# Fetching a unit of queries and keys in six transfers of 24 or 48 rows in place of twelve of 16

## The reference

```python
x = x + attn(layernorm(x))        # 16 heads, two softmaxes over 8-wide q, k; a1 @ v - lam * a2 @ v, rms norm, W_proj
x = x + xattn(layernorm(x), ctx)  # one head of 256, gelu, residual
x = x + ffn(layernorm(x))         # shared SwiGLU of 1024, and 2 of 16 routed experts of 256
```

## Time and profile before

| | |
|---|---|
| median of 3 runs | 569.85 us (569.31 to 571.27) |
| the profiled execution | 569.25 us, of which 568.0 us are the span |
| PE busy | 537.7 us (95%) |
| mean granted TensorE clock | 0.976 of 2.4 GHz |
| DVE, ACT, POOL busy | 311.8, 260.1, 228.0 us |
| queue of SP and ACT | 58,688 packets, 61.11 MB, 37.8% of 16 engines' span |

### The profile page before, as it was taken

The page is one execution under the profiler, slowest core; times in us unless marked ns, Lnnn a source line. Parts: engine busy times, 40 slices in busy tenths (PEclk is TensorE's granted clock), DMA queues, the critical chain, the costliest instruction groups (busy, mean ns, idle before and its releaser), DMA issues.

```text
span 568.0 us, 10919 instructions
## 1 busy us (share of the span) xinstructions
PE 537.7 (95%) x3792; PEld 374.1 (66%) x3792; DVE 311.8 (55%) x685; ACT 260.1 (46%) x420; POOL 228.0 (40%) x473
## 2 busy tenths in 40 slices
PE   8989878988999997799999999999999999999998
PEld 7544434645547564665585466467999999999547
DVE  5868875898898975885242762112222222222284
ACT  7335654654574664526512200102666666666110
POOL 2444766576645444523010024563244444444200
PEclk9989978999998999799999999999999999999999
DMA  7873483346431319920039806122233333332372
GB/s 238 245 177 122 116 249 92 112 124 182 135 114 43 103 55 147 310 58 0 0 112 349 281 28 211 69 90 88 75 94 95 92 90 92 95 94 83 129 280 75
DMA packets 62725, 72.99 MB, mean 129 GB/s; under 512 B 14832, under 2 KB 55792, under 8 KB 61136
## 3 DMA queue, kind: packets, MB, share of 16 engines
q1 hardware_dynamic: 58688, 61.11, 37.8%
q0 software_dynamic: 3792, 10.39, 5.2%
q10 hardware_dynamic: 192, 0.79, 0.6%
HBM read 45.84 MB, written 26.03 MB: 127 GB/s over the span
## 4 chain that ended last, share of the span: by engine, by line
PE 80%; DVE 6%; SPq 5%; ACT 3%; issue 3%; DMA 2%; POOL 1%; ACTq 0%; DVEq 0%; POOLq 0%
PE ps L671 18%; PE ps L739 15%; PE ps L682 10%; PE ps L750 7%; PE ps L399 5%; PE ps L467 3%; PE ps L595 3%; PE ps L416 2%; PE ps L455 2%; PE ps L572 2%; PE ps L548 2%; SPq L1885 2%; DVE nmax L949 2%; PE ps L695 2%; PE ps L728 2%
## 5 line engine op out<-in xcount | busy, mean ns | idle before, releaser
L949 DVE TENSOR_REDUCE nmax<-ps 128x8 f32<-128x1024 f32 x64 | 77.6, 1217 | 26.1 <-PE ps L434 24.8
L739 PE MATMUL ps<-xt,Wn 128*128 128x128 f32 x752 | 91.8, 275 | 0.1
L739 PEld LDWEIGHTS ps<-xt,Wn 128*128 128x128 f32 x752 | 87.7, 192 | 0.4 <-ACT xt L1549 0.3
L1729 POOL DMA_INDIRECT y_rows<-yo,goes_to x47 | 45.8, 975 | 82.0 <-DVE yo L1218 81.7
L1445 ACT ACTIVATE prob<-ps 128x1024 f32<-128x1024 f32 x64 | 65.4, 1021 | 24.7 <-PE ps L455 24.6
L1210 DVE TENSOR_TENSOR ht<-sa,ps 128x256 f32<-128x256 f32 x47 | 19.8, 422 | 99.2 <-PE ps L750 95.2
L1542 ACT ACTIVATE sil<-ps 128x512 f32<-128x512 f32 x32 | 19.1, 597 | 115.2 <-PE ps L671 115.2
L671 PE MATMUL ps<-xT,W1s 128*128 128x512 f32 x128 | 60.6, 596 | 1.6 <-ACT sil L1542 0.9
L671 PE MATMUL ps<-xT,W2s 128*128 128x512 f32 x128 | 60.2, 592 | 0.0
L682 PE MATMUL ps<-W3s,hTs 128*128 128x256 f32 x256 | 56.1, 380 | 0.8 <-DVE hTs L1141 0.8
L1562 ACT ACTIVATE Wn<-W 128x1024 f32 x47 | 49.7, 1057 | 12.6 <-issue 12.6
(11 more groups left out here) (186 smaller groups left out, 830.2 us busy)
## 6 DMA issues: line engine op xcount, KB each, us to landing
W<-in_L_ffn_routed_w_dram SPq DMA_DIRECT2D x12, 1024.0 KB, 11.8
pack_q<-qk_parts SPq DMA_DIRECT2D x48, 128.0 KB, 3.1
xg<-x_slots SPq DMA_DIRECT2D x47, 129.0 KB, 2.1
x_slots<-zero SPq DMA_DIRECT2D x11, 512.0 KB, 10.6
qk_parts<-part SPq DMA_DIRECT2D x21, 256.0 KB, 3.1
pack_k<-qk_parts SPq DMA_DIRECT2D x42, 128.0 KB, 3.1
yg<-y_rows SPq DMA_DIRECT2D x4, 1024.0 KB, 8.6
Cx<-in_ctx_dram SPq DMA_DIRECT2D x5, 512.0 KB, 4.3
```

Of the source, the lines that this page charges most:

```text
L739: r = t.matmul(ps[:, 2 + p, h * P:(h + 1) * P], Wn[:, n % 3, k, h * P:(h + 1) * P], xt[:, p, k, :], start=(k == 0), stop=(k == KT - 1))
L949: v.tensor_reduce(nmax[:, s % 4, a, :, :], ps[:, b:b + 2, :].rearrange("p m (h t) -> p m h t", h=4), AX_X, ALU.max, negate=True).then_inc( ...
L1729: g.indirect_dma_start(out=y_rows, out_offset=bass.IndirectOffsetOnAxis(ap=goes_to[:, n:n + 1].bitcast(U32), axis=0), in_=yo[:, p, :], in_ ...
```

## The change

The slots are laid out anew. Queries are stored as first, first, second, third part, and keys mirrored as third, second, first, first, in the slots 0 to 3. Queries' rows then are slots 0, 1, 2 and slots 1, 2, 3; keys' rows are slots 1, 2, 3 and slots 0, 1, 2, and the six products come out as before. For a group, the queries are one transfer of 48 rows whose source is a hand-built access pattern of [2 x 24 x one row], with a step of one slot in the outer dimension, so that two slots are read twice; its destination is 48 partitions. The keys of a group are two transfers of 24 rows each. A unit is fetched by 2 + 4 = 6 transfers. The first part of the queries is now stored twice, so a chunk has eight stores. The fetch is cut in `fetch_queries` and `fetch_keys`: units 3 to 7 are fetched in two steps in place of three, queries (two transfers) in the first and keys (four) in the next; unit 2 whole in step 1; the queries of unit 0 are all issued behind the second parts of half 1, ahead of its third parts.

```diff
-PARTS_AT = (((0, 1), (2, 0), (2, 2)), ((0, 2), (2, 1)), ((0, 0), (2, 3)))
-Q_RUNS = [1, 1, 0]
-K_RUNS = [0, 1, 2]
+PARTS_AT = ((0, 1), (2,), (3,))
+SLOTS, RUNS = 4, 3
-PIECES = len(Q_RUNS) + len(K_RUNS)
-FETCHES = 2 * PIECES
-STORES = 7
+FETCHES = 6
+STORES = 8
...
+        def half_of_group(pack, m, i):
+            lo = MG * m + i * RUNS * HD
+            return pack[lo:lo + RUNS * HD, :, :].rearrange("p h t -> p (h t)")
+        def keys_places(c, half, m, i):
+            return qk_parts[c, 2 + half, 1 - i:1 - i + RUNS, :, m * HU:(m + 1) * HU, :].rearrange("q d h t -> (q d) (h t)")
+        def queries_places(c, half, m):
+            first = qk_parts[c, half, 0, 0, m * HU, :]
+            return bass.AP(first.tensor, first.offset, [[HD * MU * CT, 2], [MU * CT, RUNS * HD], [1, HU * CT]])
...
-                for f0, at_ in PARTS_AT[i]:
-                    q.dma_start(qk_parts[c, f0:f0 + 2, at_, :, :, :].rearrange("f d m t -> (d m) f t"),
-                                part[PART_OF[c]][:, i, f0:f0 + 2, :]).then_inc(parts_stored[c], 16)
+                for place in PARTS_AT[i]:
+                    for f0, at_ in ((0, place), (2, SLOTS - 1 - place)):
+                        q.dma_start(qk_parts[c, f0:f0 + 2, at_, :, :, :].rearrange("f d m t -> (d m) f t"),
+                                    part[PART_OF[c]][:, i, f0:f0 + 2, :]).then_inc(parts_stored[c], 16)
...
-                            q.dma_start(tile[MG * m + r0:MG * m + KQ:3, :, :].rearrange("p h t -> p (h t)"),
-                                        qk_parts[c, f, p0:p0 + 2, :, m * HU:(m + 1) * HU, :].rearrange(
-                                            "q d h t -> (q d) (h t)")).then_inc(packed[u], 16)
+            def fetch_queries(unit):
+                c, half, u = unit // 2, unit % 2, unit % UNITS
+                may_fetch(unit)
+                for m in range(2):
+                    q.dma_start(Qp[u][MG * m:MG * m + KQ, :, :].rearrange("p h t -> p (h t)"),
+                                queries_places(c, half, m)).then_inc(packed[u], 16)
+            def fetch_keys(unit):
+                c, half, u = unit // 2, unit % 2, unit % UNITS
+                may_fetch(unit)
+                for m in range(2):
+                    for i in range(2):
+                        q.dma_start(half_of_group(Kp[u], m, i), keys_places(c, half, m, i)).then_inc(packed[u], 16)
...
-            fetch(0, range(1))
+            fetch_queries(0)
             store_half(1, 2)
-            fetch(0, range(1, len(Q_RUNS)))
             store_part(1, 0)
-            fetch(1, range(3))
+            fetch_queries(1)
             put_max(0)
-            fetch(1, range(3, PIECES))
+            fetch_keys(1)
...
-                if s in (1, 2):
-                    fetch(2, range(3 * (s - 1), 3 * (s - 1) + 3))
-                if CB <= s and s // CB + UNITS - 1 < STEPS // CB and s % CB < 3:
-                    fetch(s // CB + UNITS - 1, range(2 * (s % CB), 2 * (s % CB) + 2))
+                if s == 1:
+                    fetch_queries(2)
+                    fetch_keys(2)
+                if CB <= s and s // CB + UNITS - 1 < STEPS // CB and s % CB < 2:
+                    (fetch_queries, fetch_keys)[s % CB](s // CB + UNITS - 1)
```

More of the change, by code:

```diff
@@ L1418, in fetch_keys @@
                 a.wait_ge(halves_stored[half], 16 * STORES)
[L1419 to L1423, removed]
+                for m in range(2):
+                    for i in range(2):
+                        a.dma_start(half_of_group(Kp[unit], m, i), keys_places(0, half, m, i)).then_inc(packed[unit], 16)
             def put_values(c, i):
@@ L1859, in store_part, with may_fetch @@
                 q.wait_ge((firsts, seconds, thirds)[i], 4 * (c + 1))
-                for f0, at_ in PARTS_AT[i]:
-                    q.dma_start(qk_parts[c, f0:f0 + 2, at_, :, :, :].rearrange("f d m t -> (d m) f t"),
-                                part[PART_OF[c]][:, i, f0:f0 + 2, :]).then_inc(parts_stored[c], 16)
+                for place in PARTS_AT[i]:
+                    for f0, at_ in ((0, place), (2, SLOTS - 1 - place)):
+                        q.dma_start(qk_parts[c, f0:f0 + 2, at_, :, :, :].rearrange("f d m t -> (d m) f t"),
+                                    part[PART_OF[c]][:, i, f0:f0 + 2, :]).then_inc(parts_stored[c], 16)
             def store_half(half, i):
-                for n, (f0, at_) in enumerate(PARTS_AT[i]):
-                    f = f0 + half
+                for f, mirrored in ((half, False), (half + 2, True)):
                     q.wait_ge((firsts, seconds, thirds)[i], ORDER.index(f) + 1)
[L1868 to L1872, removed]
+                    for place in PARTS_AT[i]:
+                        at_ = SLOTS - 1 - place if mirrored else place
+                        q.dma_start(qk_parts[0, f, at_, :, :, :].rearrange("d m t -> (d m) t"),
+                                    part[0][:, i, f, :]).then_inc(halves_stored[half], 16)
+            def may_fetch(unit):
+                c, half = unit // 2, unit % 2
                 if unit < UNITS:
```

## The result

The changed kernel takes 674.77 us (median of 4 runs, 673.2 to 675.44), against 569.58 us of the kernel before (median of 4, 566.8 to 571.27): a ratio of 1.185, 95% interval 1.180 to 1.190, or 105 us more. Forecast were 640 us, in a range of 585 to 677. The direction and the mechanism were right; the growth was forecast a third too small (70 us for 105). The forecast's own range, 615 to 670, is missed by 5 us: the time lies inside the wide one only because that reached to 677 for a rival that did not come true.

What follows compares the result with a forecast made beforehand. PE bounds the kernel, busy 537.7 of 568.0 us. Stalls of 46.7 + 12.4 + 15.8 = 74.9, less 8, plus 3 for the clock, on 569.25 give 639.2, rounded to 640 us; own range 615 to 670, overall 585 to 677.

Steps and rivals of the forecast that it cites:

- Few engines: Attention fetches: a queries' transfer, (48, 2), runs on 2 engines with 24 rows each; a keys' transfer, (24, 24), on 12.
- the rival in which the transfer is cut finer: Queries' fetch: 48 rows run on 16 engines, three each, and up to 4.8 us return: 565 us; chance 0.12.
- Puts behind the queries: Attention: a put of maxima needs three engines, shares some with the queries and queues behind their 16.0 us a unit.
- the rival in which puts go by other engines: Step and put are left alone, only the units' arrival counts: 592 us; chance 0.13.
- The signs: Expected in the profile: first scores from 34 to 44, put waits from 4.8 to some 50 us in six or seven.
- The eight stalls: PE's attention waits: 46.7 us in steady state, 12.4 in unit 2, 15.8 at the start; sum 74.9.
- Needed are 1.3 + 16.0 + 0.7 = 18.0 us: Steady state: lead, queries on two engines, then the put landing, from queries' issue until the next put is usable.
- the leads: Time from a unit's first query issue to the step needing the next put: 7.6 to 12.1 us.
- The clock: PE in the attention: each long stall brings a stretch at a lower granted clock; plus 3 us in all.
- The credit: About 8 us less: 4.8 of waits falling into the stalls, and part of PE's other idle time.
- the rival with 0.43 us a row: Queries' rows cost 0.43 us in place of 0.333: +37, 677 us; chance 0.07.
- The issue gain: SP's queue: six fetches instead of twelve, 3.5 us less a unit; at most PE's 4.8 us of put waits returns.

Runs made afterwards that it cites:

- the run with three engines: Changed kernel with the queries' source pattern as three runs of 16 rows, (3, 16), and keys in six transfers to 16 neighbouring partitions: 677.05 us, ratio 1.189.
- moving them away: Changed kernel with the order in units 2 to 7 turned round, keys in the first step and queries in the next: 659.68 us, ratio 1.159.
- the repaired versions: Changed kernel with queries' transfers reshaped onto 12 or 16 engines: 575.82, 574.85 and 575.13 us; the 16-engine one spread over three steps, 571.59 us.
- the packing: Kernel before with its twelve transfers placed as the changed kernel places its own, queries in one step, keys in the next: 573.51 us, ratio 1.008.

## Why the prediction was right, and where it was too small

**Few engines: right.** From the 3 packets beyond a put's 24 followed two engines for a (48, 2) transfer. The share of 12.4% shows two, and the rival in which the transfer is cut finer (565 us) is out; changing the queries' transfers alone (24 rows by 24) brings 674.77 us down to 575.13. Twelve shows in the page of the changed kernel, in ACT's queue (packets, MB, share), which carries only the four key transfers of unit 0:

```profile
q10 hardware_dynamic: 144, 0.79, 0.4%
```

144 packets are 4 x (24 rows + 12 increments). The Trainium skill's rule (DMA: Bandwidth & Descriptors, "Why a DMA increments its semaphore by 16 and not by 1") agrees: 2 and 12 here, 3 in the share of 19.6% (3/16 = 18.8%) of the run with three engines, 16 in the earlier trace rows.

**Puts behind the queries: right.** The rival in which puts go by other engines (592 us) is out: PE's seven waits are all for the put behind a unit's queries. That they are the lowest-numbered engines no row names; that a put shares them, the waits show, and the run with the queries in ACT's queue confirms it. The signs came as forecast, but for size: PE's first scores at 44.30 us for 44, seven waits for six or seven, 87.7 us in them for some 50.

**The eight stalls, in us:**

| unit | 0 | 1 | 2 | 3 | 4 | 5 | 6 | 7 |
|---|---|---|---|---|---|---|---|---|
| forecast | 9.9 | 5.9 | 12.4 | 13.8 | 5.9 | 7.1 | 8.3 | 9.6 |
| measured | 10.1 | 9.0 | 16.0 | 15.4 | 12.1 | 9.3 | 13.2 | 12.7 |

Forecast 72.9 (74.9 with the 2 for step 16), measured 97.8. The first, where I had added up all that lay on the two engines, is right to 0.2 us, in part by luck, since 48 rows alone take 14.9 us and not the 16.0 put in. The step that was wrong by size is "Needed are 1.3 + 16.0 + 0.7 = 18.0 us": it is 21.2 us in unit 7, 21.0 in unit 4 (148.41 to 169.45) and 22.7 in unit 6 (216.96 to 239.65); for unit 2 I had 20.7, and it is 23.9 (80.56 to 104.46). The price of a row was not at fault: it is 0.31, not 0.333. What I left out is that the keys of units 4 to 7 go out 5 to 8 us behind the queries, while these still run, and can slow the two engines; in unit 2 I had counted their 2.7 us, and moving them away gave 5.0. I had written that keys cost nothing by themselves; with the keys out of the way the need is 17.9 us in unit 7, but 18.9 in units 2 and 4 and 20.0 in unit 6. With rows of 0.31 us my own sum would be 16.9, so some 1 us more stays unexplained even in unit 7. In units 3 and 5, where stores run with the queries, moving the keys gained nothing.

The second part are the leads: unit 4's was 12.1 us before and was 9.0 in the changed kernel. The lead of before contained a slow step of its own (four matmuls of L399, 3.39 us against 1.98 for the same ones in the changed kernel), which makes 1.4 of the 3.1.

**The clock: too small.** I allowed 3 us. PE is busy 186.51 us in place of 171.38, for the same instructions: +15.1. Behind a stall a stretch runs at a lower clock; from 275.5 and from 134.4 us, behind two of them (windows of the changed kernel, the third number from the end being the granted clock):

```profile
275.50:284.00 8.50, 8.47 (x79) 6.34 (x81) 4.66 (x7) 2.25 (x3) 2.39 (x8) 0.72 0.03 10
134.40:142.00 7.60, 7.15 (x57) 2.99 (x59) 3.79 (x5) 2.76 (x5) 2.20 (x5) 0.61 0.21 46
```

8.47 x (1 - 0.72) = 2.4 and 7.15 x 0.39 = 2.8 us, by estimate. Behind the other six the granted clock was 0.61 to 0.78 over the next 8 to 16 us. The kernel before had some such stretches already, so what eight stalls add is 15.1 / 8, some 2 us each. This I could have read from the earlier trace rows, where behind one stall of 2 us four matmuls took 3.32 us in place of 1.9, 1.4 more.

**The credit: about right.** PE's idle time apart from the eight waits went from 16.5 to 107.4 - 97.8 = 9.6 us, 6.9 less; I had 8.

So 97.8 - 6.9 + 15.1 = 106.0 us, the growth of the stretch, against my 74.9 - 8 + 3 = 69.9. Of the 36 missing, 23 are the stalls' length, 12 the clock. That the time still falls inside the whole range is luck: its upper end, 677, stood for the rival with 0.43 us a row, and a row took 0.31. The mechanism was the forecast one; its two terms, the need of a put and the clock, were each too small.

**The issue gain: there, and worthless,** as said. Six issues instead of twelve; the repaired versions, with six or eight, are no faster than before either. What the shorter queue gives by itself no run measures; the eighth store and the packing at least outweigh it.

## What to carry to other kernels

Count engines before transfers: for each transfer look at the outermost dimension of both sides, and put one outermost that 16 divides; 24, which gives 12 engines, was as good here. A slow transfer costs little as long as nothing urgent stands behind it; look for the small one behind it in the same queue, and compare its lead with the whole queue ahead of it, everything that other transfers put on those engines included. And a repeated stall costs its length and a stretch at a lower clock behind it, about 2 us each here.

## What the runs showed of the hardware that was not expected

- Transfers into neighbouring partitions are slow: 0.80 us a row of 8 KB, and 1.00 where transfers are densest, for 16 engines into 16 neighbours, 0.43 into every third. With keys like that in flight a row took 1.15 us in the run with three engines, whose queries take 0.36 alone. Why (a shared way into the memory, or else) was not measured.
- Between the queues of SP and ACT an engine takes turns packet by packet: 256-byte pieces each waited for one 8 KB row of 0.31 us, so another queue cured only a fifth of the wait (87.7 to 69.5 us).
- Issuing has a price by shape: a fetch of 16 rows to every third partition took 0.586 us to issue, the same to 16 neighbours 0.420 in the run of the kernel before with neighbouring partitions; in the changed kernel 24 rows on 12 engines take 0.368, and 48 on two take 0.627 (min, median, max ns of one issue):

```profile
L1896 SPq DMA_DIRECT2D pack_q<-qk_parts x16: 605/627/790, 23.1 to 255.0; - x16
L1904 SPq DMA_DIRECT2D pack_k<-qk_parts x28: 345/368/2354, 50.9 to 260.9; - x28
```
